# The second dt product and the broadcast of B as two 64-row products, issued one behind the other into two banks

## What is computed

```python
x_in = jnp.einsum('bsd,de->bse', x, w_in)
proj = jnp.einsum('bsd,dp->bsp', x_in, w_x)
dt_low, Bm, Cm = jnp.split(proj, [DT_RANK, DT_RANK + D_STATE], axis=-1)    # 64, 16, 16 columns
dt = jax.nn.softplus(jnp.einsum('bsr,rd->bsd', dt_low, w_dt) + b_dt) * (DT_MAX - DT_MIN) + DT_MIN
```

## Time and profile before

| | us |
|---|---|
| median of 3 runs | 2410.21 |
| lowest and highest | 2409.46, 2412.55 |
| span of the profiled execution | 2411.0 |

### The profile page before, as it was taken

The page is one execution under the profiler, slowest core; times in us unless marked ns, Lnnn a source line. Parts: engine busy times, 40 slices in busy tenths (PEclk is TensorE's granted clock), DMA queues, the critical chain, the costliest instruction groups (busy, mean ns, idle before and its releaser), DMA issues. The chain is left out here.

```text
span 2411.0 us, 40740 instructions
## 1 busy us (share of the span) xinstructions
PE 2080.6 (86%) x12780; PEld 1300.7 (54%) x12844; DVE 2058.5 (85%) x3846; ACT 1894.4 (79%) x3805; POOL 1185.8 (49%) x1784
## 2 busy tenths in 40 slices
PE   2438899899989989898999989899998989889887
PEld 1104546465555646465564646556465655646574
DVE  6888897989989898988989898898979889897734
ACT  4478889797878979797887979788797978867453
POOL 3004354555545455554645455454636545454744
PEclk8569899999999999999999999999999999999999
DMA  3343222313232232323223231322313132221000
GB/s 88 83 121 83 74 73 65 85 51 99 56 85 62 67 84 59 92 55 93 55 67 90 53 95 51 93 67 55 101 43 108 46 100 59 67 72 34 5 5 12
DMA packets 104435, 165.98 MB, mean 69 GB/s; under 512 B 15442, under 2 KB 34078, under 8 KB 104222
## 3 DMA queue, kind: packets, MB, share of 16 engines
q1 hardware_dynamic: 104222, 163.37, 25.4%
HBM read 146.55 MB, written 16.78 MB: 68 GB/s over the span
## 5 line engine op out<-in xcount | busy, mean ns | idle before, releaser
L1314 DVE TENSOR_TENSOR_SCAN scan_bufs<-scan_bufs,inp_bank 128x512 f32<-128x512 f32 x512 | 617.7, 1206 | 14.2 <-ACT scan_bufs L701 13.7
L1013 PE MATMUL bank<-w_gu,f_xqT 128*128 128x512 f32 x1024 | 497.5, 631 | 37.1 <-ACT f_xqT L762 35.9
L694 ACT ACTIVATE scan_bufs<-scan_bufs,a_rows 128x512 f32<-128x512 f32 x512 | 371.5, 726 | 51.1 <-DMA scan_bufs<-dt_copy 50.9
L1028 PE MATMUL bank<-w_dn,f_hqT 128*128 128x256 f32 x1536 | 357.7, 382 | 8.6 <-ACT f_hqT L762 8.6
L1013 PEld LDWEIGHTS bank<-w_gu,f_xqT 128*128 128x128 f32 x1024 | 201.5, 203 | 271.1 <-issue 267.0
L1324 DVE TENSOR_TENSOR scan_bufs<-scan_bufs,c_bank 128x512 f32<-128x512 f32 x512 | 343.1, 670 | 1.3
L701 ACT ACTIVATE scan_bufs<-scan_bufs 128x512 f32<-128x512 f32 x512 | 323.7, 632 | 3.9
L1028 PEld LDWEIGHTS bank<-w_dn,f_hqT 128*128 128x128 f32 x1536 | 284.5, 190 | 77.0 <-issue 25.7
L609 POOL TENSOR_TENSOR f_h<-f_h,f_h_scale 128x704 f32<-128x704 f32 x128 | 178.1, 1391 | 283.8 <-DVE f_h L1174 283.8
L620 POOL TENSOR_TENSOR f_h<-f_h,f_h_lean 128x704 f32<-128x704 f32 x128 | 216.1, 1688 | 124.7 <-DVE f_h L1375 116.0
L631 POOL TENSOR_SCALAR_AFFINE_SELECT masked_scores<-masked_scores 128x512 f32<-128x512 f32 x256 | 168.8, 685 | 217.6 <-ACT masked_scores L762 217.5
(11 more groups left out here) (204 smaller groups left out, 4339.5 us busy)
## 6 DMA issues: line engine op xcount, KB each, us to landing
scan_bufs<-dt_copy SPq DMA_DIRECT2D x512, 256.0 KB, 4.0
xp<-L_attn_a_x SPq DMA_DIRECT2D x16, 512.0 KB, 4.1
dt_copy<-dt SPq DMA_DIRECT2D x32, 256.0 KB, 3.0
out<-x SPq DMA_DIRECT2D x64, 128.0 KB, 3.5
w_attn<-L_attn_b_W_attn SPq DMA_DIRECT2D x1, 768.0 KB
scan_bufs<-L_ffn_w_gate SPq DMA_DIRECT2D x1, 704.0 KB
scan_bufs<-L_ffn_w_up SPq DMA_DIRECT2D x1, 704.0 KB
masked_scores<-L_ffn_w_down SPq DMA_DIRECT2D x1, 704.0 KB
```

The costliest lines, as they stand in the source:

```text
L694: nc.scalar.activation(half, half, ACT.Exp, scale=a_rows[:, c, at:at + 1]).then_inc(root_ready, 1)
L1013: last = nc.tensor.matmul(to[:, :], f.xqT[:, k, :], w_gu[:, k, g, lo:hi], start=(k == 0), stop=(k == DH - 1))
L1028: last = nc.tensor.matmul(to[:, 0:D], f.hqT[:, k, :], w_dn[:, k, :], start=(k == 0), stop=(k == FK - 1))
L1314: nc.vector.tensor_tensor_scan(half, half, inp[:, :], 0.0, ALU.mult, ALU.add)\
```

## The change

`dt1` is no longer a step of its own. The step `B` takes both banks, waiting for both to be free, then issues the product of `dt1` and right behind it that of `B`. `dt0`, `dt1`, `B` and `C` each contract over 64 rows in place of 128: the dt products over rows 0 to 63, B and C over rows 64 to 127 (the rows left out were zeros in one operand). The numbers of the shared banks stay what they were in every use. The first batch's turning of weights hangs behind `B` now, which is the same place. Nothing changes on ACT, DVE, POOL and SP.

```diff
-        ("P", "B"): 16.995, ("P", "C"): 31.245, ("P", "dt0"): 12.997, ("P", "dt1"): 17.26, ("P", "G"): 30.477,
+        ("P", "B"): 16.995, ("P", "C"): 31.245, ("P", "dt0"): 12.997, ("P", "G"): 30.477,
...
-P_USES |= {"dt0": ("dt0", "act", "abs0"), "dt1": ("dt1", "act", "abs1"), "G": ("G", "dve", "inp")}
+P_USES |= {"dt0": ("dt0", "act", "abs0"), "dt1": ("B", "act", "abs1"), "G": ("G", "dve", "inp")}
...
                 elif step == "B":
                     to, done = take("P", b, 0, step, ["low"])
-                    last = nc.tensor.matmul(to[:, :], sel_bc[:, 0, :], low[:, :], start=True, stop=True)
-                elif step in ("dt0", "dt1"):
-                    h = int(step[-1])
+                    beside, beside_done = take("P", b, 0, "dt1", ["low"])
+                    nc.tensor.matmul(beside[:, :], w_dt[0:RANK, P:2 * P], low[0:RANK, :], start=True, stop=True)\
+                        .then_inc(beside_done, 1)
+                    last = nc.tensor.matmul(to[:, :], sel_bc[RANK:P, 0, :], low[RANK:P, :], start=True, stop=True)
+                elif step == "dt0":
                     to, done = take("P", b, 0, step, ["low"])
-                    last = nc.tensor.matmul(to[:, :], w_dt[:, h * P:(h + 1) * P], low[:, :],
-                                            start=True, stop=True)
+                    last = nc.tensor.matmul(to[:, :], w_dt[0:RANK, 0:P], low[0:RANK, :], start=True, stop=True)
...
-                nc.tensor.matmul(c_rep[:, :], sel_bc[:, 1, :], low[:, :], start=True, stop=True).then_inc(c_ready, 1)
+                nc.tensor.matmul(c_rep[:, :], sel_bc[RANK:P, 1, :], low[RANK:P, :], start=True, stop=True).then_inc(c_ready, 1)
...
-                    if first(b) and step == "dt1":
+                    if first(b) and step == "B":
```

## The result

| | before | after |
|---|---|---|
| median of 12 runs, us | 2410.10 | 2416.09 |
| lowest and highest, us | 2409.11, 2413.86 | 2414.05, 2416.86 |
| ratio, 95% interval | | 1.0019 (1.0012 to 1.0026) |
| span of the profiled execution, us | 2411.0 | 2413.9 |

The changed kernel is 0.2% slower, some 6 us by the medians and 3 to 6 us by the interval. The forecast was 2423.2 us, with the loss from two sources: 3.9 us from `dt0` and 9.1 us from falls of TensorE's clock. The first came, somewhat larger; the second didn't come at all.

A forecast was written before the change was run, and what follows sets the result against it. Each batch was taken to have a longer stretch set by PE and a shorter one set by DVE. The profiled 2411.0 + 3.9 (dt0) + 9.1 (clock) = 2424.0 us, forecast as 2423.2 against the median; range 2411.5 to 2431.0.

The forecast's parts named there:

- dt0: In PE's stretch, a lone 64-row product costs 0.28 us a batch, 3.9 us over 14 batches.
- What bounds the kernel: Each 139.0 us batch has a longer stretch that PE sets and a shorter one that DVE sets.
- The pair: B and dt1 side by side take 0.99 us, and the down product behind starts 0.57 us sooner.
- rival 2: At B and dt1, the second product waits for the first; no clock fall, 2414.1 us; chance 0.10.
- Where the gain goes: PE's idle time before ACT's L738 frees a bank grows from 1.54 to 2.11 us and swallows the gain: 0.
- The clock: Behind the 2.11 us idle time TensorE's clock halves in 6.5 of 13 cases, 1.4 us each, 9.1 us.
- the first rival: TensorE's clock stays up behind the longer idle time, only dt0's cost remains, 2414.1 us; chance 0.20 (at most one fall).

The follow-up runs named there:

- dt0_whole: The changed kernel with the product of dt0 over all 128 rows again; 2411.64 us against 2410.92 of before, ratio 1.0001.
- dt0_alone: The kernel before with one edit, the product of dt0 over 64 rows; 2415.03 us, ratio 1.0015.
- all_whole: The changed kernel's order and waits with all four products over 128 rows; 2410.44 us, ratio 0.9998.
- narrow: The changed kernel with 128-row dt0, and 96 of 256 columns in the last step of the down product behind the pair; 2421.39 us against 2411.73.

## Why the prediction was wrong, step by step

**What bounds the kernel** held. PE's stretch and DVE's stretch fit the runs: 0.34 us more at `dt0` in PE's stretch counted in full, the same 64-row form at C in DVE's stretch cost nothing, and work moved ahead of an idle time of PE counted nothing.

**`dt0`** was the right mechanism, a size too small. The visit was put at 0.09 + 0.13 + 0.06 = 0.28 us. Against `dt0_whole` it measures 0.09 in front (2.79 from L1029's start to L953's, against 2.70), 0.19 up to the transposes (1.05 against 0.86) and 0.06 in them (0.71 against 0.65): 0.34. The steady batches are 0.33 us longer in `dt0_alone` than before (139.28 against 138.95) and 0.41 in the changed kernel than in `dt0_whole` (139.35 against 138.94). The term that was off is the middle one. It was read from L978, which puts eight records of 32 columns into two rounds in 0.99 us. The second record of the 64-row product, in the changed kernel, and the second round of L978, before:

```profile
751.42 0.59 PE L953 MATMUL bank<-low,w_dt 64*128 64x512 f32 x1
```

```profile
747.20 0.61 PE L978 MATMUL acc_y<-scan_bufs,sel_y 128*32 128x512 f32 x4
```

The records of one 64-row product start 0.53 us apart (751.42 - 750.89), those rounds 0.45 (747.20 - 746.75). 14 x 0.34 = 4.8 us in place of 3.9, which lies within the interval of the result.

**The pair** was right in kind (rival 2 fell: side by side) and wrong in size, and this is the step that failed. Its gain of 0.57 us was put together from a start 0.05 us behind DVE, a length of 0.99 us and nothing behind it. Measured: a start 0.15 us behind DVE's end (767.39 - 767.24), a length of 1.06, and a down product behind it of 771.14 - 768.45 = 2.69 us, where it took 772.64 - 770.05 = 2.59 (the start of L1013 in that batch of before, in the timeline, is 772.64). That is 0.10 + 0.07 + 0.10 = 0.27 us less, so the idle time grew by 0.3 and not by 0.57. The first 0.10 comes with the common wait and not with the form: in `all_whole`, with 128 rows, the first product starts 0.15 us behind DVE's end too (765.92 - 765.77), and the down product takes 770.30 - 767.71 = 2.59. The other two come with the form. The prediction had counted the slower start behind a visit (the 0.06 of the transposes) at `dt0`, and at the pair had put it inside the 0.99.

**Where the gain goes** held: ACT's Relu stayed, and the idle time took all of it.

**The clock** was a term of 9.1 us on the condition of 2.11 us of idle time, and it measured 0. The condition failed by 0.26 us, and at this place the onset lies between 1.85 and 1.95. Where the condition is all but met, `narrow` lost 9.7 us by the medians; its profiled execution, 12.3 above the median of before, had 9 falls of 1.5 us (the prediction: 6.5 of 1.4). So the case that came is the first rival, with its 2414.1, though for another reason than it gave: it said that 2.11 us might not be enough, while the idle time never was 2.11 us. I had given it 0.20. The bounds from none of 13 to all of them were stated for a length of idle time that was itself a sum of three small terms, each off by 0.1 us or less; its error should have been carried into the chance of a fall, and 1.85 us with none would then have had a larger share.

**The range**, 2411.5 to 2431.0, holds the 2416.1; the likeliest value was off because an effect that is there or not was entered at its mean size.

## What to carry to other kernels

A product over half the rows of the array saves no time alone, and costs some 0.3 us each time PE goes into that form and back; give it only to products that have a partner to run beside. Look where PE next runs dry: a gain ahead of an idle time that another engine ends is worth nothing, and may be worth less than nothing if the longer idle time lets the clock fall in a stretch that PE sets. Where a forecast hangs on such an onset, work out the error of the length before the cost of crossing it.

## What the hardware showed that I had not expected

- Leaving out 0.2 us of work a batch made the kernel 9.7 us slower (`narrow`), by halving TensorE's clock behind 9 of 13 idle times of 1.95 to 2.06 us; behind the 26 of 1.73 to 1.85 us at the same place, in the changed kernel and `dt0_whole`, it never fell.
- The product behind a visit to the array in parts starts slower: 2.69 us for the twelve records behind the pair in place of 2.59, 0.71 for the six transposes behind `dt0` in place of 0.65.
- Two 64-row products of 512 columns in different halves take 1.06 us side by side, 0.85 to 0.86 each alone with 128 rows; one alone in 64 rows takes 1.05. The second one is free, once the form is paid.
